# Three orders in the attention, and earlier transposes with joined outputs in the FFN: a fused cross-attention and MoE kernel

## The reference

```python
# x, ctx: (128, 128, 256)
def xattn(q, k, v):
    wq = (q @ wq_w.T + wq_b).reshape(b, t, 16, 16)          # the same for wk, wv
    scores = einsum('bthd,bshd->bhts', wq, wk) / sqrt(16)
    probs = softmax(scores)
    attn = einsum('bhts,bshd->bthd', probs, wv).reshape(b, t, 256)
    return attn @ wo_w.T + wo_b

def ffn(z, x):                       # z is x normalised; the gate's logits come from z too
    top1 = argmax(z @ Wg.T)          # one expert for each token
    xhat = layernorm(z)
    for e in range(8):
        h = gelu((xhat * s[e] + b[e]) @ W1[e] + b1[e])      # exact gelu
        y += (top1 == e) * (h @ W2[e] + b2[e])
    return y

x = x + xattn(layernorm(x), ctx, ctx)
x = x + ffn(layernorm(x))
```

## Time and profile before

| | |
|---|---|
| median of 3 runs | 1547.18 us (1544.44 to 1550.96) |
| the profiled execution | 1542.23 us, its span 1540.1 us |
| PE busy | 1428.5 us, 93% of the span |
| DVE, ACT, POOL busy | 77%, 56%, 28% |
| PE's chain share | 80% of the chain that ended last |
| attention | to about 1034 us, some 30.8 us a group |
| FFN | from there on, 15.8 us a group |

### The profile page before, as it was taken

How to read it: one execution, slowest core, us unless ns; L and a number is a source line. 1 busy time by engine, 2 the same in 40 slices (tenths; PEclk the granted TensorE clock), 3 DMA queues, 4 the chain that set the end, 5 groups by cost and what they waited for, 6 DMA issues and landing times.

```text
span 1540.1 us, 39587 instructions
## 1 busy us (share of the span) xinstructions
PE 1428.5 (93%) x15438; PEld 1209.1 (79%) x15438; DVE 1189.3 (77%) x2880; ACT 865.5 (56%) x1450; POOL 424.7 (28%) x602
## 2 busy tenths in 40 slices
PE   6899899999999999999989999979999999999998
PEld 5688778888888888888877887767777777777776
DVE  4788788878887888788877887767777777777775
ACT  4566666676666667766766666653333334233332
POOL 3223222322232223222322232213222232322221
PEclk9999999999999999999999999999999999999999
DMA  7566555655566556556655565411212212121211
GB/s 183 125 172 173 165 139 158 164 163 139 153 166 166 140 160 169 158 148 166 176 135 139 160 164 162 111 57 56 83 56 71 67 59 80 56 83 56 77 62 41
DMA packets 150480, 190.89 MB, mean 124 GB/s; under 512 B 17631, under 2 KB 101146, under 8 KB 150298
## 3 DMA queue, kind: packets, MB, share of 16 engines
q1 hardware_dynamic: 150298, 188.38, 44.5%
HBM read 53.01 MB, written 33.55 MB: 56 GB/s over the span
## 4 chain that ended last, share of the span: by engine, by line
PE 80%; DVE 7%; issue 6%; ACT 5%; DMA 1%; SPq 0%; ACTq 0%; DVEq 0%
PE st_ps L1215 12%; PE s_ps L1197 12%; PE pp_ps L1076 9%; PE pv_ps L1024 8%; PE st_ps L1010 7%; PE s_ps L982 7%; PE pp_ps L1084 5%; DVE negmax L733 4%; PE pp_ps L1049 4%; PE pp_ps L1070 3%; PE pv_ps L1032 3%; PE pp_ps L1163 2%; ACT pT L640 1%; PE t_ps L1001 1%; PE s_ps L1204 1%
## 5 line engine op out<-in xcount | busy, mean ns | idle before, releaser
L589 ACT ACTIVATE pT<-st_ps 128x1024 f32<-128x1024 f32 x256 | 263.2, 1028 | 164.0 <-PE st_ps L1010 164.0
L733 DVE TENSOR_REDUCE negmax<-s_ps 128x8 f32<-128x1024 f32 x256 | 311.5, 1217 | 31.8 <-PE s_ps L982 31.4
L1215 PE MATMUL st_ps<-w_hi,q_packed 128*128 128x256 f32 x1024 | 217.1, 294 | 1.9 <-DVE q_packed L844 0.9
L982 PE MATMUL s_ps<-k_packed,q_packed 96*128 96x128 bf16 x2048 | 159.1, 221 | 50.5 <-issue 40.8
L1197 PE MATMUL s_ps<-k_packed,w_hi 128*128 128x512 f32 x512 | 171.4, 423 | 18.4 <-ACT pT L640 18.4
L982 PEld LDWEIGHTS s_ps<-k_packed,q_packed 96*128 96x128 bf16 x2048 | 130.7, 98 | 70.1 <-issue 47.6
L460 POOL TENSOR_TENSOR q_parts<-q,q_parts 128x1024 bf16<-128x1024 f32 x32 | 68.5, 2139 | 418.2 <-ACT q_parts L583 418.2
L1215 PEld LDWEIGHTS st_ps<-w_hi,q_packed 128*128 128x128 f32 x1024 | 168.1, 188 | 14.6 <-DVE q_packed L844 8.4
L632 ACT ACTIVATE offhotT<-pv_ps 96x512 bf16<-96x512 bf16 x31 | 18.4, 593 | 253.8 <-PE pv_ps L1184 253.8
L1010 PE MATMUL st_ps<-q_packed,k_packed 98*128 98x128 bf16 x2048 | 158.8, 220 | 0.2
L1215 PE MATMUL st_ps<-w_lo,q_packed 128*128 128x256 f32 x512 | 142.9, 279 | 0.0
(11 more groups left out here) (180 smaller groups left out, 3480.9 us busy)
## 6 DMA issues: line engine op xcount, KB each, us to landing
q_packed<-q_parts SPq DMA_DIRECT2D x192, 256.0 KB, 3.8
k_packed<-k_parts SPq DMA_DIRECT2D x192, 256.0 KB, 4.5
xin<-in_x_dram SPq DMA_DIRECT2D x32, 512.0 KB, 3.8
cin<-in_ctx_dram SPq DMA_DIRECT2D x32, 512.0 KB, 3.9
x_scratch<-xb SPq DMA_DIRECT2D x32, 512.0 KB, 4.7
xin<-x_scratch SPq DMA_DIRECT2D x32, 512.0 KB, 4.6
out_dram<-xb SPq DMA_DIRECT2D x32, 512.0 KB, 3.2
q_packed<-negmaxT SPq DMA_DIRECT2D x128, 8.0 KB
```

The lines of the kernel that those rows point to most:

```text
L589: a.activation(pT[u % 2][:], st_ps[:], ACT.Exp, scale=DH ** -0.5).then_inc(s_exp, 1)
L733: v.tensor_reduce(own, s_ps[:].rearrange("p (h s) -> p h s", s=P), AX_X, ALU.max, negate=True).then_inc(s_red, 1)
L982: mm = t.matmul(s_ps[:, j * P:(j + 1) * P], packed[0][n % 2][0:KP, slot(m, j), tok], packed[1][n % 2][0:KP, slot(m, j), tok], start=True, ...
L1215: t.matmul(o, h[n % 2][:, m, tok].bitcast(F32R), w[:, m, :].bitcast(F32R), start=(m == 0 and k == 0), stop=False)
```

## The change

In the attention:

- SP issues the last part of the keys' pack before the store of x2, and not behind it.
- ACT keeps item 0 of group n + 2 before the exponential of unit 4, and not behind it.
- DVE at unit 6 takes the maxima first, then the lower part of item 3, then the rest of the attention output; before, these two stood ahead of the maxima, in the other order.

In the FFN:

- PE's eight transposes for the next group stand behind the second mask, ahead of `hidden(n, 2)`.
- PE's outputs of sequences 0 and 1 are joined: blocks 0 to 2 of both, then block 3 of both. The gate stands behind them.
- ACT keeps the transposes between the second and the third gelu, and copies the next group's `xb` behind the fourth.
- DVE's statistics of group n + 2 stand ahead of the splits of the hidden layer, but for group 0.
- SP issues the load of group n + 3 in group n, with group 2 ahead of the loop.

```diff
@@ ffn_sync, on SP
             def group(n):
-                if n + 2 <= LAST:
-                    ffn_load(sp, n + 2)
+                if n + 3 <= LAST:
+                    ffn_load(sp, n + 3)
                 store(n)
 
+            ffn_load(sp, 2)
             for n in range(GROUPS):
                 group(n)
@@ attention, group(g) on SP
+                if g < LAST:
+                    pack(g + 1, 1, 2)
                 if g > 0:
                     store_x2(g - 1)
-                if g < LAST:
-                    pack(g + 1, 1, 2)
                 load_max(g, 3)
@@ attention, group(n) on ACT
+                    if more2 and u == 4:
+                        item(n + 2, 0)
                     if more2 and u == 6:
                         item(n + 2, 3)
                     exp(n, u)
...
                     for ahead, k in SLICES[u]:
-                        if n + ahead <= LAST and k != 3:
+                        if n + ahead <= LAST and k not in (0, 3):
                             item(n + ahead, k)
@@ ffn_group on ACT
-                for m in range(MC):
-                    gelu(n, m)
-                    if m == 0 and n == 0:
-                        act.wait_ge(st_x2[0], 8 * GROUPS)
-                        copy(0)
-                    if m == 1:
-
-                        a.copy(onehotT[n % 2][:], onehotT_ps(n))
-                    if m == 1 and n < LAST:
-                        if n == 0:
-                            act.wait_ge(st_x2[1], 8 * GROUPS)
-                        copy(n + 1)
+                gelu(n, 0)
+                if n == 0:
+                    act.wait_ge(st_x2[0], 8 * GROUPS)
+                    copy(0)
+                gelu(n, 1)
+                a.copy(onehotT[n % 2][:], onehotT_ps(n)).then_inc(f_oh, 1)
                 if n < LAST:
                     for c in range(C):
                         keep_xT(n + 1, c)
+                for m in range(2, MC):
+                    gelu(n, m)
+                if n < LAST:
+                    if n == 0:
+                        act.wait_ge(st_x2[1], 8 * GROUPS)
+                    copy(n + 1)
@@ attention, group(n) on DVE
-                    if more2 and u == 6:
-                        rest_of_attn(*done)
-                        lower(n + 2, 3)
                     if done and u % 2 == 1:
                         norm(*done)
                     if later(n, u, 3):
                         maxima(*later(n, u, 3))
+                    if more2 and u == 6:
+                        lower(n + 2, 3)
+                        rest_of_attn(*done)
@@ ffn_group on DVE
+                if 0 < n <= LAST - 2:
+                    ffn_stats_of(dve, n + 2)
                 for m in range(MC):
                     split_hidden(n, m)
-                if n + 2 <= LAST:
-                    ffn_stats_of(dve, n + 2)
+                if n == 0:
+                    ffn_stats_of(dve, 2)
@@ turn on PE
                     pe.wait_ge(s_x2, GROUPS * GB)
-                    pe.wait_ge(f_he, 3)
+                    pe.wait_ge(f_oh, 1)
@@ output on PE
-            def output(n, b):
+            def output(n, b, parts):
...
-                wait(pe, f_out, at(GB, n, b - 1))
-                for m in range(MC):
+                if parts[0] == 0:
+                    wait(pe, f_out, at(GB, n, b - 1))
+                for m in parts:
...
-                t.matmul(o, onehotT[n % 2][:, tok], b2p[:], start=False, stop=True).then_inc(f_y, 1)
+                if parts[-1] == MC - 1:
+                    t.matmul(o, onehotT[n % 2][:, tok], b2p[:], start=False, stop=True).then_inc(f_y, 1)
@@ ffn_group on PE
                     mask(n, 0)
                     mask(n, 1)
+                if more:
+                    for c in range(C):
+                        turn(n + 1, c)
                 for m in range(2, MC):
                     hidden(n, m)
                     mask(n, m)
+                for parts in (range(MC - 1), range(MC - 1, MC)):
+                    for b in range(2):
+                        output(n, b, parts)
                 if more:
-                    for c in range(C):
-                        turn(n + 1, c)
-                for b in range(GB):
-                    output(n, b)
-                    if b == 1 and more:
-                        gate(n + 1)
-                    if b == 2 and more:
-                        turn_logits(n + 1)
+                    gate(n + 1)
+                output(n, 2, range(MC))
+                if more:
+                    turn_logits(n + 1)
+                output(n, 3, range(MC))
```

More of the change, by code:

```diff
@@ L252, in xattn_moe @@
         f_gl, f_gle = sem("ffn_logitsT_in_psum"), sem("ffn_logitsT_kept")
+        f_oh = sem("ffn_onehot_kept")
         GK = 5
```

## The result

| | before | after |
|---|---|---|
| median of 4 runs, same chip | 1547.69 us (1544.44 to 1550.96) | 1475.97 us (1474.65 to 1476.46) |
| ratio, 95% interval | | 0.9535 [0.9514, 0.9556] |
| span of the profiled execution | 1540.1 us | 1473.9 us |
| span up to PE's first onehot transposes (L1184, now L1190) | 1029.1 | 988.9 |

The change makes the kernel 72 us faster; 1483 was forecast, with a range of 1456 to 1507. Of the 66.2 us by which the span shrinks, 40.2 lie ahead of the first onehot transposes, in the attention, and 26.0 behind them, in the FFN (37 and 27 forecast).

The account below looks back on a forecast made before the run. PE, busy for 93% of the span, was taken as the bound, with its idle time to be won. Attention 37 us plus FFN 27 us made 64 us: 1547.2 - 64 = 1483 us, range 1456 to 1507.

Parts of the forecast that it names:

- the three rows: PE's waits once a group: 40.8 us scores (nothing shown), 15.0 us transposed maxima, 18.4 us third hidden block for the gelu.
- The pack's landing: Attention: the last keys' pack, issued before the store, lands 2.1 us earlier (bounds 0.64 and 2.1); the scores' wait, costing 1.49, goes.
- late pack: Rival: the landing moves only with its issue, 0.64 us; 1496 us, or 1510 with half the FFN gain; chance 0.2 together.
- The store 1.0 us later: Attention: the x2 store behind the pack lands 1.0 us later, near 530.0, so POOL's four bias additions start about S + 1.2.
- S: Start of the first scores of an attention group on PE; forecast to come 1.1 to 1.5 us earlier.
- DVE and POOL meet: Attention: DVE's two small instructions behind the maxima wait for POOL's bias additions, 0.8 us a group, bounds 0 and 1.3.
- my rival: DVE and POOL hardly meet: 24 us more won in the attention, 1459 us; chance 0.18.
- ACT's item 0: Attention: the cast ahead of unit 4's exponential lets DVE's residual end at 529.6, so PE's item 1, wanted at 529.9, doesn't wait.
- Attention's sum: Per attention group: 1.49 us for the first wait less 0.25 for later transposed maxima, 1.24; 37 us in 30 groups.
- the 0.98 worked out: FFN gain in us a group from moved transposes and joined outputs; less 0.08 for POOL's small instructions, 0.90, 27 us in 30.
- slower: Rival: FFN statistics ahead of the splits let a late load hold up splits and outputs; 1576 us at 11 us landings; chance 0.03.
- Group 0: First FFN group: its transposes wait for the onehot copy, which stands behind a 1 us copy; gives 1 us back.

## Why the prediction was right, step by step

- **What bounds the kernel: right, overstated.** PE's idle time is what was won. But the three rows hold 74 of the 112 us that PE stands idle (1540.1 less 1428.5), not nearly all of it.
- **The place and sign of the three waits: right.** All three shrank as said, in the kernel and in the runs with one order alone.
- **The pack's landing: mis-sized; what it brings: right in the main.** 2.1 us was the estimate, with 0.64 as the other bound; it moved by 1.16, of which 0.90 is the earlier issue. So the bytes ahead counted for 0.27 us, of an estimated 1.5. The scores gained 1.10 a group where 1.49 was taken, and a rest of 8.7 us in 14 waits stays, where I had said under 5 in all. The rival "late pack" had the mechanism nearly right and the size wrong: it let 0.85 of each wait stand, since it counted 0.64 for the issue.
- **The store 1.0 us later: by two errors.** In the group shown it lands 1.4 us later (5.39 and then 6.79 after the issue of the first of the last three packs), and S comes 0.83 earlier and not 1.1. POOL starts at S + 1.27 for the S + 1.2 forecast because the two cancel.
- **DVE and POOL meet: right on DVE, mis-sized on PE.** Priced at 0.8, measured 0.88 in this group and 0.67 on average. But PE's way to the transposed maxima lost only about 0.3 by it. They came at S + 7.68 in this group, not S + 7.85; without the meeting S + 7.3 and not S + 7.05. ACT's casts of items 1 and 3 hold DVE at nearly the same time, so "no slack" was the wrong step. This is why holding POOL back brings 4 to 5 us and not the 24 of my rival.
- **ACT's item 0: right.** The prediction said that the residual's wait "doesn't appear"; without the order it does, and costs 21 us together with what follows it. What the prediction lacked is that size, so it couldn't say how much hung on this step. The second scores, forecast 2.39 behind the first, come 2.17 behind them (512.30 to 514.47), so nothing is given back there. It isn't a term of the sum.
- **Attention's sum: 1.24 a group forecast, 1.33 measured** (30.84 to 29.51 from one group's first scores to the next one's, mean of 29). The first scores gave 1.10 where 1.49 was taken. The transposed maxima came 0.29 earlier on average (S + 7.85 to S + 7.56), where 0.25 later was taken. Some 0.16 of that 0.29 comes from the clock: three groups of the kernel before have the transposed maxima at S + 9.1 to 9.2, where the median is S + 7.56, and each holds a stretch at half clock (see the last section). The prediction had no term for it.
- **FFN: right.** 0.99 a group for the 0.98 worked out; the 0.08 that I took off for POOL's small instructions wasn't lost. The join is worth over 30 us with the transposes moved. The rival "slower" has nothing for it: from the second FFN group on, PE waits once, 0.6 us, so no load came late.
- **Group 0: mis-sized.** 1 us forecast, 4.5 measured; the wait is 3.2 us and a stretch of half clock follows. It was weighed as one transpose's lateness, not as an idle stretch.

The time came out at 1476, 7 us from the forecast. The errors are of opposite signs (landing 0.4 a group too good, the way to the transposed maxima 0.5 a group too dear, the FFN from its second group on 2 to 3 us too low and its first group 3.5 too good), so a part of the closeness is luck.

## What to carry to other kernels

A wait taken away uncovers the next one: the pack's order alone turned 33 us of idle time into 16 us of gain, and the transposes' move without the join would have lost. So price each order by what is due next on the same engine, and try orders together where each covers the other's new wait. Time won on an engine that feeds the bound is worth only what lies on the bound's path (0.3 of 0.67 us a group here): follow it to the bound's next instruction before it goes into a sum.

## What the runs showed of the hardware that was not expected

- **TensorE's clock after an idle stretch.** PE sat idle for 3.24 us at the start of the FFN, and the granted clock then averages 0.74 over 13 us: part of it at 1.2 GHz, with the matmul pair at 1.20 us and not 0.71. All eight profiles with a stop of 3.2 us there have a stretch at half clock there, of 3.4 or 6.8 us; none of the six without it has.
- **The clock also fell at long waits for the landing.** In the kernel before, one such stretch begins 0.7 us after scores (at 315.17) that had waited 1.76 us:

```profile
315.90:319.30 3.40, 3.40 (x24) 3.19 (x21) 2.67 (x5) 2.36 (x4) 1.09 (x2) 0.50 0.23 59
```

  The three profiles with the pack behind the store have 11 such stretches in the attention after the first 60 us, each from 0.3 us before to 1.6 us after scores that had waited 1.76 to 2.18 us. Not each such wait has one: there are 19 of them. The eleven profiles with the pack ahead have one stretch there between them, and their waits for a landing reach 1.75 us once and 1.5 else. Each cost the kernel before about 1.5 us. No run set out to test this.
- **Of DVE and POOL, the one that starts second is held up.** In the FFN before, POOL works first, and DVE's small `first` is stretched to 1.15 us (0.19 alone), until POOL's work (1203.78 and 1.29) has ended:

```profile
1203.98 1.15 DVE L817 TENSOR_TENSOR first<-hit,rank 128x32 f32<-128x32 f32 x1
```

  With the change POOL's work is over before `first` comes, and this takes 0.19 in every group, as the view by line shows (shortest, median and longest in ns):

```profile
L821 DVE TENSOR_TENSOR first<-hit,rank x32: 191/193/193, 988.2 to 1455.0; 128x32 f32<-128x32 f32 x32
```

  POOL's own work now starts 0.17 us behind an instruction of DVE (L857, 1155.78 to 1156.46) and is stretched instead, from 1.29 to 1.68. Only one weight load ever waits for it, 0.5 us:

```profile
1155.95 1.68 POOL L518 TENSOR_TENSOR k_packed<-k,k_packed 128x512 fp32r<-128x512 f32 x1 [3.59 <-DVE k_packed L854]
```

- **A store of 512 KB ahead of a pack of 256 KB on the same queue** made the pack's way from its issue to its landing 0.27 us longer (4.70 against 4.43 us, means of 30 groups), beside 0.90 us by which the pack was issued later. A store behind it delays it by no more than 0.1 us (4.43 and 4.40 with it, 4.31 without).
